# A fused Mamba block and feed-forward on one NeuronCore: the sums of dt times a from pairs of fp16 products instead of fp32 ones

## What is computed

```python
dt = jax.nn.softplus(dt_toks + dt_bias)          # 8 heads
dA = jnp.exp(dt * A)                             # A = -exp(A_log)
def step(S, inp):
    dA_t, dt_t, B_t, C_t, x_t = inp
    S = S * dA_t[:, :, None, None] + jnp.einsum('bh,bn,bhp->bhpn', dt_t, B_t, x_t)
    y_t = jnp.einsum('bhpn,bn->bhp', S, C_t)
    return (S, y_t)
...
h = jax.nn.silu(gate) * up                       # weights are lut[idx]
return _ghost_linear(h, down_idx, lut)
```

## Time and profile before

| what | value |
|---|---|
| three runs | 1440.67, 1443.71, 1446.11 us |
| the profiled execution | 1443.4 us |
| its span, first to last instruction | 1441.7 us |
| mean granted TensorE clock | 0.982 |
| TensorE busy (matmul) | 1361.3 us, 94% of the span |
| VectorE busy | 933.8 us, 65% |
| ScalarE busy | 577.1 us, 40% |
| GpSimd busy | 457.6 us, 32% |
| DMA | 87.79 MB, mean 61 GB/s |

### The profile page before, as it was taken

One profiled execution on the slowest core, in us unless ns is written; L12 is line 12 of the kernel. 1 busy time (PEld: TensorE's weight loads), 2 busy tenths in 40 slices (PEclk: granted clock), 3 DMA queues, 4 the chain that ended last, 5 costly groups with the idle time before them and its releaser, 6 DMA issues. The chain is left out here.

```text
span 1441.7 us, 19103 instructions
## 1 busy us (share of the span) xinstructions
PE 1361.3 (94%) x6912; PEld 672.6 (47%) x6912; DVE 933.8 (65%) x1869; ACT 577.1 (40%) x1018; POOL 457.6 (32%) x691
## 2 busy tenths in 40 slices
PE   4878987988999999999999999999999999999998
PEld 2334444444554445444545445544554444444443
DVE  7978866987577656765676567755775555544432
ACT  5466655676444234332434243423442233122120
POOL 1312233333233434334322433254334242310102
PEclk9889998999999999999999999999999999999999
DMA  5133233322310223013301320032102110311201
GB/s 164 37 102 88 69 93 100 92 75 56 74 45 23 59 70 85 19 36 93 73 16 52 88 71 26 23 92 77 44 23 71 39 44 23 97 43 30 74 1 51
DMA packets 99021, 87.79 MB, mean 61 GB/s; under 512 B 68208, under 2 KB 68208, under 8 KB 98928
## 3 DMA queue, kind: packets, MB, share of 16 engines
q1 hardware_dynamic: 97040, 86.54, 21.8%
q10 hardware_dynamic: 1888, 0.03, 0.1%
HBM read 54.05 MB, written 16.78 MB: 49 GB/s over the span
## 5 line engine op out<-in xcount | busy, mean ns | idle before, releaser
L1312 PE MATMUL bank<-fxt,ffn_hi 128*128 128x512 f16 (+1 forms) x1408 | 418.8, 379 | 2.0 <-DVE dn L1677 1.5
L1312 PE MATMUL bank<-fxt,ffn_lo 128*128 128x512 f16 (+1 forms) x704 | 266.8, 379 | 0.0
L1312 PEld LDWEIGHTS bank<-fxt,ffn_hi 128*128 128x128 f16 (+1 forms) x1408 | 139.8, 100 | 173.1 <-issue 12.9
L1210 PE MATMUL bank<-mask,diag 128*128 128x416 f16 x640 | 128.0, 354 | 21.7 <-ACT ffn_lo L830 20.2
L605 POOL TENSOR_TENSOR state<-state,ex 64x512 f32<-64x512 f32 x32 | 36.8, 1149 | 343.3 <-PE bank L1265 342.3
L1326 PE MATMUL bank<-ffn_hi,h_hi 128*128 128x512 f16 (+1 forms) x352 | 133.5, 379 | 0.0
L1326 PE MATMUL bank<-ffn_hi,h_lo 128*128 128x512 f16 (+1 forms) x352 | 133.4, 379 | 0.0
L1326 PE MATMUL bank<-ffn_lo,h_hi 128*128 128x512 f16 (+1 forms) x352 | 133.3, 379 | 0.0
L1643 DVE SCALAR_TENSOR_TENSOR gact<-gact,bank 128x512 f32<-128x512 f32 (+1 forms) x88 | 60.2, 684 | 105.7 <-ACT gact L874 104.8
L874 ACT ACTIVATE gact<-bank,c_gate_half 128x512 f32<-128x512 f32 (+1 forms) x88 | 59.9, 681 | 154.7 <-PE bank L1312 153.1
L1496 DVE TENSOR_SCALAR mask<-codes_h 128x832 f16<-128x832 f16 x320 | 111.7, 408 | 12.5 <-PE bank L1210 12.2
(11 more groups left out here) (184 smaller groups left out, 2357.3 us busy)
## 6 DMA issues: line engine op xcount, KB each, us to landing
codes_sb<-codes SPq DMA_DIRECT2D x80, 208.0 KB, 3.4
ures<-u SPq DMA_DIRECT2D x32, 256.0 KB, 2.8
x_scratch<-x SPq DMA_DIRECT2D x32, 256.0 KB, 2.0
ut<-x_scratch SPq DMA_DIRECT2D x16, 512.0 KB, 4.3
xres<-x_scratch SPq DMA_DIRECT2D x32, 256.0 KB, 3.0
out<-dn SPq DMA_DIRECT2D x32, 256.0 KB, 2.1
ut<-u SPq DMA_DIRECT2D x15, 512.0 KB, 4.4
ffn_hi<-w_in_t SPq DMA_DIRECT2D x4, 580.0 KB, 9.2
```

The source lines that it names most:

```text
L1210: last = nc.tensor.matmul(p.bank[:, 0:COLS], diag[:, q].rearrange("p n m -> p (n m)"), mask[:, n, q, j * COLS:(j + 1) * COLS], start=(q == ...
L1312: last = nc.tensor.matmul(bank, wt[:, c0:c0 + w], fxt[:, :, half, k, :], start=(k == 0 and n == 0), stop=(k == KC - 1 and n == 2))
```

## The change

dt times a is multiplied by 2^8 (in a, at the start), held above -60000, and split in an fp16 high part and an fp16 low part; the exponentials divide by 2^8 again. GpSimd makes two products in fp16, high and low, in the place of `decay`; their 2 x 1024 fp16 numbers fill the same bytes. TensorE adds both in PSUM. The masks for these sums are fp16 copies; `below` in fp32 is kept only at the start, in the memory of y.

```diff
--- before.py
+++ after.py
@@ -64,6 +64,10 @@
 TINY = 2.0 ** -60
 HSCALE = 2.0 ** -54
 
+
+SEG = 2.0 ** 8
+SEG_LOW = -60000.0
+
 Place = namedtuple("Place", "bank filled freed n")
 
 
@@ -161,8 +165,9 @@
         ffn_lo = sb("ffn_lo", [P, WCOLS], F16)
         ident = sb("ident", [P, P])
         causal = sb("causal", [P, P])
-        below = sb("below", [P, P])
-        ones = sb("ones", [P, P])
+        causal_h = sb("causal_h", [P, P], F16)
+        below_h = sb("below_h", [P, P], F16)
+        ones_h = sb("ones_h", [P, P], F16)
         neg_half = sb("neg_half", [P, SUB])
         lut_sb = sb("lut_sb", [P, CODES])
         conv_w_sb = sb("conv_w_sb", [P, FB, TAPS])
@@ -210,7 +215,7 @@
         dtp = sb("dtp", [P, SUB, HEADS])
         dt = sb("dt", [P, SUB, HEADS])
         dt4 = sb("dt4", [P, 2, SUB, HEADS])
-        da = sb("da", [P, 2, SUB, HEADS])
+        da = sb("da", [P, 2, SUB, 2, HEADS], F16)
         xs = sb("xs", [P, 2, KC, TILE])
         bs = sb("bs", [P, TILE])
         cs = sb("cs", [P, TILE])
@@ -309,11 +314,11 @@
         conv_steps = Signal(sem("conv_steps"), FB * CSTEPS)
         ctanh_ready = Signal(sem("conv_tanh_ready"), FB)
         xs_ready = Signal(sem("conv_silu_ready"), FB + 1)
-        dt_steps = Signal(sem("dt_steps"), 18)
+        dt_steps = Signal(sem("dt_steps"), 21)
         dt_exp = Signal(sem("dt_exponential"), 1)
 
         ztanh_ready = Signal(sem("z_tanh_ready"), SUB)
-        seg_ready = Signal(sem("segment_terms_ready"), SUB)
+        seg_ready = Signal(sem("segment_terms_ready"), SUB * 2)
         xtok_done = Signal(sem("x_tokens_transposed"), SUB)
         seg_done = Signal(sem("segment_sums_done"), SUB)
         xtok_ready = Signal(sem("x_tokens_ready"), SUB)
@@ -352,6 +357,9 @@
         res_stored = [Signal(sem(f"output_stored{i}"), SUB // 2, step=16, credit=True) for i in range(2)]
 
         xsplit_flat = xsplit[:].rearrange("p s n d -> p (s n d)").bitcast(F32)
+
+        segs = decay[:].rearrange("p h t -> p (h t)").bitcast(F16).rearrange("p (n h t) -> p n h t", n=2, h=HEADS)
+        below = y[:, 0:P]
 
         def place(t, name):
             b, n = place_of[t, name]
@@ -566,16 +574,17 @@
                     if t > 0 or c > 0:
                         pool.wait_ge(y_done.sem, y_done.now(t, c))
                     if c == 0:
-                        pool.wait_ge(dt_steps.sem, dt_steps.now(t, 17))
-                    seg_ready.inc(nc.gpsimd.tensor_tensor(
-                        decay[:], causal[:].unsqueeze(1).broadcast_to((P, HEADS, P)),
-                        da[:, t % HALVES, c, :].unsqueeze(2).broadcast_to((P, HEADS, P)), ALU.mult))
+                        pool.wait_ge(dt_steps.sem, dt_steps.now(t, 20))
+                    for n in range(2):
+                        seg_ready.inc(nc.gpsimd.tensor_tensor(
+                            segs[:, n], causal_h[:].unsqueeze(1).broadcast_to((P, HEADS, P)),
+                            da[:, t % HALVES, c, n, :].unsqueeze(2).broadcast_to((P, HEADS, P)), ALU.mult))
 
                 def weights(t, c):
                     pool.wait_ge(xtok_ready.sem, xtok_ready.now(t, c + 1))
                     pool.wait_ge(y_steps.sem, y_steps.prev(t, YSTEPS * (SUB + c - 1) + 3))
                     if c == 0:
-                        pool.wait_ge(dt_steps.sem, dt_steps.now(t, 18))
+                        pool.wait_ge(dt_steps.sem, dt_steps.now(t, 21))
                     xdt_ready.inc(nc.gpsimd.tensor_tensor(
                         xdt[:].rearrange("p (h d) -> p h d", h=HEADS),
                         xtok[:].rearrange("p (h d) -> p h d", h=HEADS),
@@ -702,8 +711,8 @@
 
                 nc.gpsimd.memset(ident[:], 0.0).then_inc(s_fill, 1)
                 nc.gpsimd.memset(causal[:], 1.0).then_inc(s_fill, 1)
-                nc.gpsimd.memset(below[:], 1.0).then_inc(s_fill, 1)
-                nc.gpsimd.memset(ones[:], 1.0).then_inc(s_fill, 1)
+                nc.gpsimd.memset(below, 1.0).then_inc(s_fill, 1)
+                nc.gpsimd.memset(ones_h[:], 1.0).then_inc(s_fill, 1)
                 nc.gpsimd.memset(neg_half[:], -0.5).then_inc(s_fill, 1)
                 nc.gpsimd.memset(eps_c[:], EPS).then_inc(s_fill, 1)
                 nc.gpsimd.memset(neg_one[:], -1.0).then_inc(s_fill, 1)
@@ -714,7 +723,7 @@
                                         base=0, pattern=[[-1, P]], channel_multiplier=1).then_inc(s_const, 1)
                 nc.gpsimd.affine_select(out=causal[:], in_=causal[:], compare_op=ALU.is_ge, fill=0.0,
                                         base=0, pattern=[[1, P]], channel_multiplier=-1).then_inc(s_const, 1)
-                nc.gpsimd.affine_select(out=below[:], in_=below[:], compare_op=ALU.is_gt, fill=0.0,
+                nc.gpsimd.affine_select(out=below, in_=below, compare_op=ALU.is_gt, fill=0.0,
                                         base=0, pattern=[[-1, P]], channel_multiplier=1).then_inc(s_const, 1)
                 pool.wait_ge(s_const, 3)
                 pair_rstd("u", 0, 0)
@@ -842,14 +851,15 @@
                     p = place(t - 1, "sN") if c == 0 else place(t, f"s{c}")
                     act.wait_ge(p.filled, p.n + 1)
                     sums_ready.inc(nc.scalar.activation(
-                        ex[:], p.bank[:, 192:216].rearrange("p (k h) -> p k h", k=3), ACT.Exp))
+                        ex[:], p.bank[:, 192:216].rearrange("p (k h) -> p k h", k=3), ACT.Exp, scale=1.0 / SEG))
                     nc.scalar.activation(gram[:], p.bank[:, 0:P + NST], ACT.Copy).then_inc(p.freed, 1)
 
                 def decays(t, c):
                     act.wait_ge(seg_done.sem, seg_done.now(t, c + 1))
                     for n in range(2):
                         decay_ready.inc(nc.scalar.activation(
-                            decay[:, 4 * n:4 * n + 4, :], seg_banks[n][:].rearrange("p (h t) -> p h t", h=4), ACT.Exp))
+                            decay[:, 4 * n:4 * n + 4, :], seg_banks[n][:].rearrange("p (h t) -> p h t", h=4), ACT.Exp,
+                            scale=1.0 / SEG))
 
                 def y_transposed(t, c):
                     p = place(t, f"y{c}")
@@ -1238,20 +1248,22 @@
                     p = take(t - 1, "sN") if c == 0 else take(t, f"s{c}")
                     nc.tensor.matmul(p.bank[:, 0:P], bs[h, tok], cs[h, tok], start=True, stop=True)
                     nc.tensor.transpose(p.bank[:, 128:192], bs[h, tok], ident[h, h])
-                    pe.wait_ge(dt_steps.sem, dt_steps.now(t, 17))
-                    for n, sums in enumerate((causal, below, ones)):
-                        last = nc.tensor.matmul(p.bank[:, 192 + n * HEADS:192 + (n + 1) * HEADS], sums[:],
-                                                da[:, half, c, :], start=True, stop=True)
+                    pe.wait_ge(dt_steps.sem, dt_steps.now(t, 20))
+                    for n, sums in enumerate((causal_h, below_h, ones_h)):
+                        for piece in range(2):
+                            last = nc.tensor.matmul(p.bank[:, 192 + n * HEADS:192 + (n + 1) * HEADS], sums[:],
+                                                    da[:, half, c, piece, :], start=(piece == 0), stop=(piece == 1))
                     last.then_inc(p.filled, 1)
 
                 def segment_sums(t, c):
-                    pe.wait_ge(seg_ready.sem, seg_ready.now(t, c + 1))
+                    pe.wait_ge(seg_ready.sem, seg_ready.now(t, 2 * c + 2))
                     if t > 0 or c > 0:
                         pe.wait_ge(y_steps.sem, y_steps.prev(t, YSTEPS * (SUB + c - 1) + 2))
                     for n in range(2):
-                        last = nc.tensor.matmul(seg_banks[n][:], below[:],
-                                                decay[:, 4 * n:4 * n + 4, :].rearrange("p h t -> p (h t)"),
-                                                start=True, stop=True)
+                        for piece in range(2):
+                            last = nc.tensor.matmul(seg_banks[n][:], below_h[:],
+                                                    segs[:, piece, 4 * n:4 * n + 4, :].rearrange("p h t -> p (h t)"),
+                                                    start=(piece == 0), stop=(piece == 1))
                     seg_done.inc(last)
 
                 def scan(t, c):
@@ -1563,7 +1575,10 @@
                     chain(dt_steps, i, 16, nc.vector.scalar_tensor_tensor(
                         dt[:], dtx[:], 0.0, dtp[:], ALU.max, ALU.add))
                     chain(dt_steps, i, 17, nc.vector.tensor_tensor(
-                        da[:, p], dt[:], a_sb[:].unsqueeze(1).broadcast_to((P, SUB, HEADS)), ALU.mult))
+                        dtp[:], dt[:], a_sb[:].unsqueeze(1).broadcast_to((P, SUB, HEADS)), ALU.mult))
+                    chain(dt_steps, i, 18, nc.vector.tensor_scalar(dtp[:], dtp[:], SEG_LOW, None, ALU.max))
+                    chain(dt_steps, i, 19, nc.vector.tensor_copy(da[:, p, :, 0, :], dtp[:]))
+                    chain(dt_steps, i, 20, nc.vector.tensor_sub(da[:, p, :, 1, :], dtp[:], da[:, p, :, 0, :]))
```

(4 more changed lines are left out.)

## The result

The changed kernel takes 1435.57 us (median of 14 runs, 1433.14 to 1438.92); the kernel before, on the same chips, 1444.51 us (14 runs, 1438.12 to 1447.49). The ratio is 0.9941, with a 95% interval of 0.9928 to 0.9954: 8.5 us faster. The profiled execution took 1435.94 us, its span 1433.8 us. The forecast was 1430.

The account below looks back on a forecast made before the run. TensorE was taken to bound the kernel from 360 to 1215 us, with no single engine setting the pace in decoding. The sum was 1443.4 - 19 + 4.2 + 1 = 1430 us, range 1409 to 1444.

Parts of the forecast that it names:

- TensorE's block: Causal and segment sums of each chunk: 1.03 us in place of 2.49, some 1.44 us saved per chunk.
- GpSimd: Two fp16 segment products per chunk at 1.9 us each, 1.9 us on top; TensorE would not wait for the second.
- The lock: GpSimd's second product holds VectorE's steps with two inputs in SBUF; low half of h 1.4 us late.
- Chunk 2: Sums of chunk 2, stages 2 to 6: TensorE waits 2.0 us for VectorE's gate product, five times, 10 us.
- Chunk 1: Sums of chunk 1: VectorE's wait for the u load makes TensorE wait 0.8 us, 4 us in five stages.
- The steady part: From 360 to 1215 us, where TensorE sets the pace: 33 - 10 - 4 = 19 us saved.
- Start: First chunk: later segment product offset by faster records, VectorE's convolution held; +1 us, bounds -1 and +3.
- Decoding: Chunks 1 to 8, feed-forward weights decoded: VectorE's delays outweigh the saving, +4.2 us, bounds -11.5 and +15.
- The clock: TensorE's granted clock in decoding: no term for a change; a lower clock was counted only at the start.
- the clean win: Rival: the second product holds nobody or is quick; 1408 us, from 1400 to 1418; chance 0.2.
- The absorbed case: Rival: the saving returns as waits for VectorE, decoding at +15; 1450 us, or 1440 with one part; chance 0.22.
- The slower case: Rival: VectorE becomes the bound at block 7's bank in the dt-chain chunk; 1462 us, milder 1451; chance 0.1.

Follow-up runs that it names:

- the run with one product: Changed kernel, but GpSimd makes only the high product, TensorE reads it twice and the exponential halves the sum; low piece left out: 1422.78 us.
- the fillers: Unread extra TensorE products in the decoding stages: 1433.35 us in the changed kernel, 1426.19 us in that kernel with both parts in one 32-bit product.
- the sums thrice: Segment products made three times in the first nine chunks: 1410.85 us in the one-pair-product kernel with both edits, 1438.89 us in the changed kernel.
- both edits: Changed kernel with one 32-bit pair product, dt*a split on GpSimd without the -60000 bound, and VectorE's u-load wait behind gate block 2: 1412.50 us.

## Why the prediction was right, and where it was off

- **TensorE's block.** Predicted 1.03 us in place of 2.49, measured 1.02; windows without a wait are 1.46 us shorter, predicted 1.44. Right.
- **GpSimd.** Predicted 1.9 us for each product, measured 1.90; and TensorE waits for none but the first. Right. Fp16 operands and output gain GpSimd nothing here (1895 ns, against 1896 in the earlier trace rows).
- **The lock.** The low half of h was to lose 1.4 us beside the second product; it lost 1.2 (0.66 to 1.87). In the run with one product it takes 0.66 us again. The convolution in this chunk was held for 0.7 us where 1.0 was expected. By the Trainium skill (SBUF — State Buffer, Who interferes with whom) the two engines exclude each other at a shared pair of ports; these rows agree.
- **Chunk 2.** Predicted five waits of 2.0 us from the second product, the convolution and the dt chain; measured 1.7 to 1.8 in the windows, and 1.5 to 1.65 as idle time. One product takes away 1.1 (the second product, with the convolution behind it), the chain's three steps off VectorE the rest. Right, each part shown by its own run.
- **Chunk 1.** Predicted waits of 0.8 us from the load of u; measured 0.65 in four windows (0.48 us where TensorE's timeline shows one as idle time) and 1.7 (1.5 as idle time) in the last stage that has a next tile, where 0.8 was predicted too. That last one is no trait of the change: with the fillers and with the sums thrice it is 0.5 us, as in the other stages. Moving the load's wait takes all of it. Right.
- **The steady part.** Predicted 19 us, measured 20.4.
- **Start.** Predicted +1, measured +0.7 at the first chunk. TensorE waits 7.4 us for the first product, 4.00 before.
- **Decoding.** Predicted +4.2 us, measured +11.8 (12.5 less 0.7). This is the term that was mis-sized, and with 7.6 us it makes more than the 5.6 us between forecast and result; the steady part's 1.4 us hid some of it, by luck. By the prediction's three groups: the two chunks where TensorE waits for the split y, predicted 2.8 us, measured 0.5; the two with the dt chain, predicted 1.4, measured 2.8; and the other four, "1.44 us saved stand against 1.4 us: 0", measured 8.4, of which 8.0 are the sums of chunk 3 of tiles 0 and 1. The step that failed is the last one. It is not that the saving counted for less: in these four windows the waits took back 6.2 us for 5.8 saved, so that pair does come to nought, though mostly by waits for ScalarE's results. What the nought left out is that the products which stay may run slower: TensorE's remaining work took 8.0 us longer there.
- **The clock.** The prediction put it at nothing in decoding, and gave no reason. From the first scan to that of tile 2, saved work, waits and slower products make -11.5 + 12.1 + 11.1 = 11.7 of the 11.8 us. The kernel before with the second product twice lost 4.4 us to waits and 7.8 to slower products there, and with three dt steps 1.7 and 8.9, so neither needs the saving. Over the traces of all fourteen kernels here the window with chunk 3's sums of tile 1 goes by the clock, whatever was edited: 37.6 us at a granted clock of 1.00, 38.8 at 0.96 to 0.97, 40.1 at 0.92, and 42.2 to 42.8 at 0.87 to 0.88. What stays open is why the lower level lasts longer. In tile 0 it begins, in both traces, within 0.7 us of TensorE taking up work after 3.56 us without any; in the kernel before it then lasts 3.4 us (139.8 to 143.3 us), after the change 10.2 us (141.6 to 151.8 us), and TensorE is busy through both. It also varies between executions of one kernel: the kernel before took 1438.19 us in one at 0.988 and 1451.98 at 0.977. So part of the sums above is the execution that was profiled; but the medians of the executions, 0.981 for the kernel before and 0.973 for the changed one, say the same: some 12 us of full-speed time.
- **What the saving is worth there.** The runs with the sums made thrice show that 15.7 us more of TensorE's work cost 0 and 3.3 us, so taking 11.5 us away can hardly have won much. Put into the kernel before, the second product alone costs 12.3 us of the median and the three steps 6.7, and in their profiled executions all of it lies ahead of the steady part.

Of the rivals, the clean win fell with the lock. The absorbed case came true in one half: decoding lost 12 of its 15 us, but for another reason. The slower case never came near: VectorE has 588 us of work in 855.

## What to carry to other kernels

A saving on the busiest engine counts only in the stages where that engine sets the pace; put a multiple of the saved work back in the other stages, and its price tells what the saving is worth there, if the granted clock stays the same. In a stage with waits, compare how long the same products take before and after, and not the waits alone: here the waits took back the saving, and what was lost on top was the clock's. Where a shortened engine now catches up with another, find each wait's own last link: two small moves (a wait for a load behind the step that frees a bank, two small steps on an idle engine) and one product instead of two gave 23 us on top of the change's 8.5. Of these 23 us some lie in decoding and were not explained one by one. Before an engine does a product twice for two fp16 parts, look whether it may carry both in one 32-bit word.

## Not expected

- The best version, with both edits, takes 1412.50 us against 1445.56 before, a ratio of 0.9773. It lacks the bound at -60000 on 256 times dt times a, so it holds only for inputs that stay within fp16's range.
- Three steps on 32 numbers per partition, some 0.7 us each time, cost 5 us by the ratio (1.0036) and 6.7 by the medians, with waits of TensorE only 1.6 us longer.
- An fp16 operand with every other number left out costs TensorE 10 ns per product of 512 columns (387 against 377 ns), not a second pass.
- One kernel's executions differ with its clock: the one with the sums thrice took 1419.42 us at 0.974 and 1409.57 at 0.984.
